# DLRM tower on one core: the first loads, the waits, and the pair products of tiles 0 and 1 carried to their rows through a DRAM scratch tensor

## The reference, cut to what matters

```
e = stack([tbl_f[ids[:, f]] for f in range(26)], axis=1)      # 512 x 26 x 128
combined = concat([dense[:, None, :], e], axis=1)             # 512 x 27 x 128
inter = einsum('bnd,bmd->bnm', combined, combined)[:, triu]   # 512 x 351
h = concat([dense, inter, dense], axis=1)                     # 512 x 607
h = relu(h @ W_top1 + b_top1)                                 # 512 x 512
h = relu(h @ W_top2 + b_top2)                                 # 512 x 256
y = h @ W_top3                                                # 512 x 1
```

## Time and profile before

| what | value |
|---|---|
| median of three runs | 116.22 us |
| the profiled execution's own time | 116.31 us |
| its span, first to last instruction | 114.2 us |
| mean granted PE clock | 0.97 of full speed |
| PE / DVE / ACT / POOL busy | 102.1 / 83.6 / 64.4 / 65.2 us |

### The profile page before, as it was taken

How to read it: one execution, slowest core, us unless ns; L and a number is a source line. 1 busy time by engine, 2 the same in 40 slices (tenths; PEclk the granted TensorE clock), 3 DMA queues, 4 the chain that set the end, 5 groups by cost and what they waited for, 6 DMA issues and landing times.

```text
span 114.2 us, 3925 instructions
## 1 busy us (share of the span) xinstructions
PE 102.1 (89%) x1605; PEld 75.6 (66%) x1605; DVE 83.6 (73%) x251; ACT 64.4 (56%) x136; POOL 65.2 (57%) x69
## 2 busy tenths in 40 slices
PE   5975799999997999999999899999799986599981
PEld 2323587675684768889399778959677635567870
DVE  3069997999999997999999998999242660336021
ACT  0099949979999999857944920596500312001210
POOL 0777776877777777777777777777675000000000
PEclk9999859999999999999999999999999999859999
DMA  2689995999677457832933822121122000000000
GB/s 39 202 247 381 364 309 99 317 346 335 130 279 234 136 137 235 274 110 52 252 116 70 287 82 52 52 67 47 46 56 69 1 0 6 6 0 6 6 0 1
DMA packets 10239, 15.55 MB, mean 136 GB/s; under 512 B 2466, under 2 KB 6366, under 8 KB 10222
## 3 DMA queue, kind: packets, MB, share of 16 engines
q1 hardware_dynamic: 8142, 11.04, 31.0%
q0 software_dynamic: 2080, 4.26, 13.5%
HBM read 15.29 MB, written 0.00 MB: 134 GB/s over the span
## 4 chain that ended last, share of the span: by engine, by line
PE 59%; DVE 15%; ACT 13%; issue 7%; DMA 3%; SPq 1%; ACTq 0%; DVEq 0%
PE turn_ps L559 11%; PE turn_ps L560 10%; PE gram_ps L583 10%; PE h_ps L661 8%; DVE onehot_sb L795 7%; PE h_ps L629 6%; PE turn_ps L543 5%; DVE low_sb L804 3%; DMA lookup_ids_sb<-in_lookup_ids 3%; ACT onehot_sb L737 3%; PE h_ps L616 3%; ACT high_sb L715 3%; ACT onehot_sb L730 2%; PE place_ps L600 2%; ACT feats L687 2%
## 5 line engine op out<-in xcount | busy, mean ns | idle before, releaser
L518 POOL DMA_INDIRECT rows_sb<-in_tbl,ids_sb x65 | 65.0, 1000 | 22.0 <-issue 19.5
L795 DVE TENSOR_SCALAR_CACHE_REDUCE onehot_sb<-lookup_ids_sb,row_ids_sb 128x512 fp32r<-128x512 int16 (+2 forms) x78 | 45.2, 627 | 3.4 <-DMA lookup_ids_sb<-in_lookup_ids 3.4
L559 PE MATMUL turn_ps<-onehot_sb,high_sb 128*128 128x512 f32 (+2 forms) x108 | 41.2, 390 | 3.0 <-DVE low_sb L807 1.8
L560 PE MATMUL turn_ps<-onehot_sb,low_sb 128*128 128x512 f32 (+2 forms) x108 | 37.2, 354 | 0.0
L559 PEld LDWEIGHTS turn_ps<-onehot_sb,high_sb 128*128 128x128 f32 x108 | 20.7, 192 | 10.6 <-issue 3.7
L730 ACT ACTIVATE onehot_sb<-lookup_ids_sb,row_ids_sb 128x512 fp32r<-128x512 int16 (+2 forms) x30 | 18.6, 638 | 6.9 <-PE turn_ps L560 6.9
L560 PEld LDWEIGHTS turn_ps<-onehot_sb,low_sb 128*128 128x128 f32 x108 | 20.8, 193 | 2.0 <-issue 0.5
L804 DVE TENSOR_TENSOR low_sb<-table_sb,high_sb 128x512 fp32r<-128x512 f32 (+2 forms) x24 | 16.4, 689 | 1.7 <-ACT high_sb L715 1.2
L583 PE MATMUL gram_ps<-feats 128*32 128x27 f32 x960 | 12.6, 197 | 4.0 <-issue 3.0
L737 ACT ACTIVATE onehot_sb<-onehot_sb 128x512 fp32r<-128x512 f32 (+2 forms) x30 | 15.5, 544 | 0.0
L583 PEld LDWEIGHTS gram_ps<-feats 128*32 128x32 f32 x960 | 10.9, 112 | 6.9 <-issue 4.4
(11 more groups left out here) (51 smaller groups left out, 71.5 us busy)
## 6 DMA issues: line engine op xcount, KB each, us to landing
table_sb<-in_tbl SPq DMA_DIRECT2D x12, 256.0 KB, 4.3
table_sb<-in_tbl SPq DMA_DIRECT2D x6, 320.0 KB
lookup_ids_sb<-in_lookup_ids SPq DMA_DIRECT2D x12, 128.0 KB, 4.1
table_sb<-in_tbl SPq DMA_DIRECT2D x6, 192.0 KB, 5.2
rows_sb<-in_tbl,ids_sb POOLq DMA_INDIRECT x65, 4.4
w1p_sb<-in_w_pairs SPq DMA_DIRECT2D x1, 768.0 KB, 7.6
w1d_sb<-in_w_dense SPq DMA_DIRECT2D x1, 512.0 KB, 6.7
w_sb<-in_w SPq DMA_DIRECT2D x1, 512.0 KB, 6.9
```

Of the source, the lines that this page charges most:

```text
L518: pool.indirect_dma_start(out=rows_sb[:, GATHERS.index((tile, slot)), :], out_offset=None, in_=tables[f], in_offset=bass.IndirectOffsetOnAxis(
L559: nc.tensor.matmul(bank, high_sb[0:rows, u % 2, c, :], picked, start=c == 0, stop=False)
L560: nc.tensor.matmul(bank, low_sb[0:rows, u % 2, c, :], picked, start=False, stop=c == CHUNKS[u] - 1).then_inc(chunk_used, 1)
L795: nc.vector.tensor_scalar(onehots(u, [c])[:, 0, :], lookup_ids_sb[:, u % TABLE_BUFS, LOOKUP_FROM[u] * P:B], row_ids_sb[:, row:row + 1], No ...
```

## The change

- The row ids of all chunks go behind the sample ids in one tensor and one DMA; the separate load (`rid`) goes. DVE and ACT wait for that one DMA.
- The ids of table 0 for the one-hots are loaded from ACT's own queue ahead of everything, and all such ids lie 128 times in DRAM (one copy a partition), where one row was broadcast. `w3` and `b2` are laid out like that too.
- ACT runs one dummy activation on zeros before its first step.
- `table_split` no longer waits for the cast; the waits for many copies are joined to one for each engine; two waits in `place_out` and `merge` go.
- PE's matmuls on zeros go from 18 to 12.
- Tiles 0 and 1 have no `place` and no copies: the last addition of `merge` writes to `folds`, SP writes it to a scratch tensor in DRAM (`fold`, one DMA of 128 rows of 1536 bytes) and reads it back (`spread`, four DMAs, one a target quadrant, three of 32 rows and one of 31, in pieces of 384 bytes) into `spread_pairs`, whose last quadrant DVE has set to 1.0. `layer1` takes that as its weights, a third of the elements each.
- Tile 3 is placed in two parts, where there were three.
- All four orders are written anew.

```
-WARM_UPS = 18
+WARM_UPS = 12
...
 SP_ORDER = """
-    ids; rid; table 0; id; table 1; dn; w1p; table 2; table 3; table 4; w1d; mask; sm; w2; table 5; table 6;
-    table 7; table 8; table 9; table 10; table 11
+    ids; table 0; id; table 1; dn; table 2; w1p; table 3; sm; table 4; table 5; mask; table 6; table 7; w1d;
+    table 8; table 9; w2; fold 0; table 10; spread 0; table 11; fold 1; spread 1
...
+            load_lookup_ids(nc.scalar, 0)
+            act.wait_ge(zeros_made, 1)
+            nc.scalar.activation(table_warm_sb[:, :], zeros_sb[:, 0:1], ACT.Abs)
...
+            def fold_out(tile):
+                i = SPREAD_TILES.index(tile)
+                sp.wait_ge(merged, done("dve", "merge", tile, *gram_parts(tile)[-1]))
+                sp.dma_start(folds_dram[i], folds[:, i, :, :, :].rearrange("p to g s -> p (to g s)")).then_inc(
+                    folds_written[i], 16)
+
+            def spread(tile):
+                i = SPREAD_TILES.index(tile)
+                if i == 0:
+                    sp.wait_ge(bias_ready, 3)
+                sp.wait_ge(folds_written[i], 16)
+                by_vec = folds_dram[i].rearrange("(q row) (to x) -> to row q x", q=QUADS, to=QUADS)
+                for to in range(QUADS):
+                    rows = NPAD if to < QUADS - 1 else BIAS_ROW - to * NPAD
+                    sp.dma_start(
+                        spread_pairs[to * NPAD:to * NPAD + rows, i, :, :].rearrange("p (q g) s -> p q (g s)", q=QUADS),
+                        by_vec[to, 0:rows]).then_inc(pairs_spread[i], 16)
...
+                if tile in SPREAD_TILES:
+                    held = spread_pairs[:, SPREAD_TILES.index(tile), :, :].rearrange("p b s -> p s b")
+                    pe.wait_ge(pairs_spread[SPREAD_TILES.index(tile)], 16 * QUADS)
...
+                if tile in SPREAD_TILES:
+                    low, high = (side.rearrange("p (s to) g -> p s to g", to=QUADS) for side in (low, high))
+                    at = folds[:, SPREAD_TILES.index(tile), :, groups, :].rearrange("p to g s -> p s to g")
+                nc.vector.tensor_tensor(at, low, high, ALU.add).then_inc(merged, 1)
```

More of the change, by code:

```diff
@@ L217, in place_parts @@
 def place_parts(tile):
-    return gram_parts(tile) if tile == TILES - 1 else [(0, GROUPS)]
+    if tile < TILES - 1:
+        return [(0, GROUPS)]
+    return [(first, first + ROUND_GROUPS) for first in range(0, GROUPS, ROUND_GROUPS)]
+SPREAD_TILES = range(0, 2)
 PE_ORDER = """
-    lookup 0 0:7; turn 0 0; lookup 0 7; lookup 1 0:8; lookup 2 0:6; turn 0 1; lookup 2 6:8; lookup 3 0:5; turn 0
-    2; lookup 3 5:8; lookup 4 0:3; turn 0 3; lookup 4 3:8; turn 0 4; lookup 5 0:3; turn 1 0; lookup 5 3:8;
@@ L230 @@
[L230 to L234, removed]
+    lookup 0 0:8; lookup 1 0; turn 0 0; lookup 1 1:8; lookup 2 0:8; turn 0 1; lookup 3 0:2; turn 0 2; lookup 3
@@ L239 @@
[L239 to L248, removed]
@@ L249 @@
-    cast 11 1; onehot 10 9; onehot 11 7; distance 11 8:10; copy turn 2 1; onehot 11 8:10; copy lookup 10; copy
-    turn 2 3; copy lookup 11; twin 3; turned1 1 0 4; place 2 0 32; copy turn 3 1; copy turn 3 3; turned1 2 0 4;
-    place 3 0 16; place 3 16 24; place 3 24 32; relu1 3 0 2; turned1 3 0 2
+    distance 0 6; cast 0 0; distance 0 7; cast 0 1; onehot 0 6; distance 1 5; cast 1 0; distance 1 6; onehot 0
+    7; cast 1 1; distance 1 7; copy lookup 0; onehot 1 5; distance 2 6; onehot 1 6; cast 2 0; onehot 1 7; copy
@@ new lines @@
+    turn 0 0; distance 2 7; cast 2 1; cast 3 0; onehot 2 6:8; distance 3 5:7; copy lookup 1; distance 3 7;
+    onehot 3 5:7; cast 3 1; distance 4 6; copy turn 0 1; copy lookup 2; distance 4 7; cast 4 0; onehot 3 7;
+    onehot 4 6; cast 4 1; copy turn 0 2; copy lookup 3; cast 5 0; cast 5 1; distance 5 5; onehot 4 7; onehot 5
+    5; distance 5 6:8; dense; copy lookup 4; onehot 5 6; cast 6 0; onehot 5 7; copy turn 0 4; copy turn 0 3;
+    cast 6 1; distance 6 8:10; cast 7 0; cast 7 1; onehot 6 8; twin 0; copy lookup 5; distance 7 7; onehot 6 9;
@@ new lines @@
+    distance 7 8:10; onehot 7 7; distance 8 8; onehot 7 8:10; onehot 8 8; copy turn 1 1; cast 8 0; distance 8 9;
+    onehot 8 9; cast 8 1; distance 9 7; copy lookup 6; copy lookup 7; distance 9 8; cast 9 0; onehot 9 7; copy
+    turn 1 3; distance 9 9; cast 9 1; copy lookup 8; cast 10 0; distance 10 8; twin 1; twin 2; onehot 9 8;
+    distance 10 9; cast 10 1; onehot 9 9; copy turn 2 1; distance 11 7; cast 11 0; distance 11 8; copy lookup 9;
+    onehot 10 8; twin 3; turned1 0 0 4; onehot 10 9; cast 11 1; onehot 11 7; copy lookup 10; onehot 11 8;
@@ L252 @@
+    distance 11 9; onehot 11 9; copy turn 2 3; copy lookup 11; turned1 1 0 4; copy turn 3 1; place 2 0 32; copy
+    turn 3 3; turned1 2 0 4; place 3 0 16; place 3 16 32; relu1 3 0 2; turned1 3 0 2
 """
 DVE_ORDER = """
-    onehot 0 0:2; low 0 0; onehot 0 2:6; low 0 1; onehot 1 0:3; low 1 0; onehot 1 3:5; low 1 1; onehot 2 0; low
-    2 0; onehot 2 1:3; low 2 1; onehot 2 3:6; onehot 3 0:2; low 3 0; low 3 1; onehot 3 2:5; onehot 4 0:3; low 4
-    0; low 4 1; onehot 4 3:6; onehot 5 0; low 5 0; onehot 5 1:4; low 5 1; onehot 5 4; dense; onehot 6 0; low 6
@@ L258 @@
[L258 to L262, removed]
@@ L427, in wait_copied, with wait_all_copied @@
             engine.wait_ge(copied[by], done(by, "copy", *fill))
+        def wait_all_copied(engine, fills):
+            for by in copied:
+                if counts := [done(by, "copy", *fill) for fill in fills if fill_copier(fill) == by]:
+                    engine.wait_ge(copied[by], max(counts))
         def run(engine, own):
@@ L441, in table_split @@
         def table_split(engine, u, part):
-            engine.wait_ge(high_split, done("act", "cast", u, part))
             engine.wait_ge(low_split, done("dve", "low", u, part))
@@ L592, in place @@
                 pe.wait_ge(merged, done("dve", "merge", tile, *last_merge))
[L593 to L596 removed]
+                if tile - 1 not in SPREAD_TILES and first == 0:
+                    pe.wait_ge(placed_dve, done("dve", "place", tile - 1, *place_parts(tile - 1)[-1]))
+                    pe.wait_ge(placed_act, done("act", "place", tile - 1, *place_parts(tile - 1)[-1]))
                 for q in range(QUADS):
@@ L825, in merge @@
                                             (end - 1) // HALF_GROUPS % 2))
-                if first == 0 and tile > 0:
+                if first == 0 and tile > 0 and tile - 1 not in SPREAD_TILES:
                     dve.wait_ge(place_done, done("pe", "place", tile - 1, *place_parts(tile - 1)[-1]))
```

112 lines of the change are left out of this document (61 added, 51 removed).

## The result

The changed kernel takes 120.1 us (median of 4 runs, 119.94 to 120.47), the kernel before 116.26 us beside it (116.21 to 116.46): a ratio of 1.033, with a 95% interval of 1.030 to 1.036. The forecast was 113.5 us, and the time lies above its range. The profiled execution took 120.47 us with a span of 118.7, 4.5 us longer than the span before.

The account below looks back on a forecast made before the run. DVE was taken to set the pace ahead of 57 us, PE after it; -2.1 - 0.7 - 1.4 - 0.4 - 0.5 - 0.2 + 2.6 = -2.7 us gave 113.5 us against the median, the forecast's own range 111.3 to 115.6.

Parts of the forecast that it names:

- Late pairs: Layer 1 of tiles 0 and 1: PE waits 2.3 and 0.3 us for pairs through DRAM, +2.6 us.
- the one-engine case: Scratch reads: a single DMA engine carries the last read's 31 rows, +2.3 us, time 118.5; chance 0.23.
- Start: Kernel start: ids issued earlier and one one-hot fewer ahead of the second low part, -2.1 us.
- its low clock: PE from 13.5 to 17 us: the half-clock stretch doesn't come, -0.7 us, bounds 0 and -1.75, or +1.75.
- the third rival: Start: PE, not DVE, holds the kernel from early on, start gives 0.9, time 116.0; chance 0.10.
- At nothing: Parts costed at zero: weight and mask loads later on SP's queue, merge's strided write, weights' spacing, tables 10 and 11.
- Place: Tiles 0 and 1 without placing: PE saves 0.80 us each, DVE and ACT a copy; -1.4 us together.
- waits: PE's sequencer at tiles 1 and 3: one wait an engine saves 0.2 us each, -0.4 in all.
- twins: PE's standstill under ACT's twin copy at 81.15 us (0.74) shrinks in the new order, -0.5 us.
- tile 3: Tile 3 placed in two parts, with the bias matmul filling a wait, -0.2 us.
- rival two: Tile 3's products: the 2.08 us pause and half-clock behind it go, another 3.8 us, time 109.7; chance 0.20.
- the two signs of being wrong: PE waits over 3 us at both tiles, or DVE's earlier start finds PE in its way.

Follow-up runs that it names:

- e1: The changed kernel with the last scratch read of 31 rows cut into 16 and 15: 115.95 us, ratio 0.990 to the kernel before.
- e9: The changed kernel with the last read cut into 16 and 15 rows and the first gathered rows turned behind lookup 1: 114.28 us, ratio 0.986.
- e12: The changed kernel with the last read cut into 16 and 15 rows, first turn behind lookup 1, ids loaded apart: 115.68 us, ratio 0.991.
- e4: The kernel before with the new start alone (ids, dummy activation, 12 warm-ups): 115.32 us, ratio 1.002.
- e2: The changed kernel with the first gathered rows turned behind lookup 1: 118.93 us, ratio 1.030 to the kernel before.
- e6: The kernel before with the new start and the first turn behind lookup 1: 183.24 us on a slower chip, ratio 0.998.
- e7: The kernel before with half of tile 2's layer 2 moved between tile 3's products: 184.04 us on a slower chip, ratio 1.002.
- e8: The kernel before with new start, first turn behind lookup 1, half of tile 2's layer 2 between tile 3's products: 184.03 us on a slower chip.
- e10: The kernel before with the new start and PE's first turn behind lookup 1, on a third chip: 116.56 us, ratio 1.006.
- e11: The kernel before with the new start, but sample ids alone first on SP and row ids on ACT's queue: 115.26 us, ratio 0.988.
- e3: The changed kernel with the pairs of tiles 0 and 1 placed by PE again: 119.16 us, no ratio given.

## Why the prediction was wrong

**Late pairs (+2.6 forecast): the step that failed.** The forecast took a read's landing as 2.0 to 4.1 us, over all engines, and put the one-engine case beside it with 0.23. That case is what happened: landings of 6.09 and 4.54 us. The pairs of tile 0 are ready at T + 9.8 (54.46 and 64.25) and those of tile 1 at T + 8.0 (80.9 and 88.9), where the forecast had 7.6 and 5.5 and the rival 9.3 for tile 0. The term is 4.23 + 1.44 of waits and 2.55 of low clock at tile 0, 8.2 us in place of 2.6. The rival's sum was near by luck: it had 3.6 for tile 1, where 1.44 was measured, and named the low clock without a price. With the read cut the forecast's own numbers nearly come out: ready at T + 7.6 (e1), 7.2 (e9) and 8.2 (e12) at tile 0 with waits of 1.54, 1.21 and 2.63 (2.3 forecast); at tile 1 no wait in e1 and e12 and 1.25 in e9 (0.3 forecast).

**Start (-2.1) and its low clock (-0.7).** DVE gained more than forecast: 3.1 us (11.96 - 8.22 = 3.7, less the 0.67 of one one-hot). The forecast then counted DVE's gain as the kernel's, although PE's next work but one, the first gathered rows, hangs on no engine that the change makes faster. In every kernel that waits for them PE goes on with them between 14.0 and 14.8 us; PE stands 3.46 us for them here, and runs at 0.50 from 16 to 19, about as long as it had from 13.5 to 17: the low clock moved and didn't go. e4 measures the whole term: nothing, within about 1 us. It is the third rival (head start lost), but with a DMA in the way and not PE's own load.

**At nothing: the orders.** I costed the moved steps one by one and the turn of the first rows not at all. It stands one chunk after lookup 0 in the new order. What moving it is worth isn't told apart from the scatter: 0.4 to 1.3 us alone (e2), and on top of the split 1.8 by e9 (e1's median is 0.15 over its kernel before, e9's 1.62 under) but 0.4 by e12 (0.22 under), which has it too. The lookups bear a gain out up to lookup 8, which ends 1.9 us earlier in e9 and 2.1 in e12 than in e1. `merge` of tile 0 is another reordering: it ends at 54.46 in place of 50.43, its first half at 48.90 in place of 46.54, and between the halves DVE now has `dense` too and a wait of 0.98 for ACT's cast. The forecast counts all from T, the end of `merge`, and so put nothing on T itself being 4.0 us later; whether an earlier T would hide some of the wait wasn't tried.

**Place (-1.4), waits (-0.4), twins (-0.5), tile 3 (-0.2).** PE has 3.8 us less of work: two placings of 0.8, six warm-ups (2.0) and less time at 1.2 GHz in the tail, against 2.55 more in layer 1 of tile 0. None of these terms was measured alone. Their sum can be seen only in e9: with the two faults mended its span is 111.5, the very number of the forecast's sum, but that is luck, since the start gives less, and the pause below is nearly gone (0.61).

**The pause (rival two).** The forecast kept it, with 0.20 for its going. It went but for 0.33: the tail from the end of layer 1 of tile 1 has full clock, and between the start of tile 3's products and the end PE needs 14.3 us (101.92 to 116.2) in place of 16.7 (95.13 to 111.8), 2.4 less. Its place is a count. In before, e4, e6, e7, e8, e10 and e11 the pause stands behind 2753 of PE's recorded instructions (weight loads, matmuls and semaphore events); the kernel after has its 0.33 behind the same 2753, and e3 has its two pauses behind 1473 and 3009, which is 5 x 256 less and 256 more. Ahead of each a packet of 16 KB starts in an instruction queue, and PE goes on 2.3 to 2.9 us after that start: 96.0 and 98.39 in before, 103.4 and 105.84 in after. In before PE had 0.3 us of work left when the packet started; in after it had 2.1, with layer 2 and transposes between tile 3's products. So the place is a count, while the length goes with how long PE's instructions ahead of the place last. That is what the rival said in other words, and e7 doesn't speak against it. No run changed the one without the other, and what starts the packet stays open.

Of the two signs of being wrong neither came to the letter: PE waited over 3 us at one tile only (1.44 at the other), and what DVE's earlier start found in its way was a transfer, not PE. The reads, with the clock behind them, cost 5.6 us more than forecast; the start's two terms of 2.8 came to nothing; one gain of 2.4 wasn't counted: -2.7 + 5.6 + 2.8 - 2.4 = +3.3, where the span shows +4.5. The start's term is known from e4 to about 1 us only, and the 1.2 that is left isn't explained.

## What to carry to other kernels

Look at the row count of every DMA that something waits for, and try a number like 31 in parts: a read of 31 rows landed 2.6 us later than reads of 16 and 15, for one issue more. Before an early start is credited, look for the next instruction in order that waits for a transfer, and see when that lands; a pause moved there costs its length and the lowered clock behind it. And count PE's instructions when a step goes: here the pauses with the releaser "issue" stood a multiple of 256 recorded instructions apart, so one can come, go or move with a removed step, and slower work ahead of such a place went with a shorter one.
